# Layer 0's edge pass: one-hot selections built in pairs of tiles from bf16 locations

## The reference

```python
h = x @ W_w + W_b
row, col = (edge_index[0], edge_index[1])
e = h[row] @ a_src + h[col] @ a_dst + a_b
e = jax.nn.leaky_relu(e, negative_slope=0.01)
attention = jax.nn.softmax(e, axis=0)
out = jax.ops.segment_sum(attention * h[col], row, num_segments=N_NODES)
```

## Time and profile before

| | us |
|---|---|
| median of three runs (11213.9 to 11227.5) | 11218.07 |
| profiled execution, its time | 11216.49 |
| profiled execution, span of the core | 11214.7 |
| first weigh of the pass / last half of a weigh, starts | 2893.7 / 3919.0 |

### The profile page before, as it was taken

How to read it: one execution, slowest core, us unless ns; L and a number is a source line. 1 busy time by engine, 2 the same in 40 slices (tenths; PEclk the granted TensorE clock), 3 DMA queues, 4 the chain that set the end, 5 groups by cost and what they waited for, 6 DMA issues and landing times. The chain is left out here.

```text
span 11214.7 us, 161449 instructions
## 1 busy us (share of the span) xinstructions
PE 7016.7 (63%) x46023; PEld 5941.3 (53%) x46024; DVE 6329.4 (56%) x14524; ACT 2694.6 (24%) x4442; POOL 5210.9 (46%) x5267
## 2 busy tenths in 40 slices
PE   0034334443567658878787456666666588888885
PEld 0033333333466646666666334444444588888885
DVE  8932222222577766666666444444445566666665
ACT  5022222222455532222222132222222100000000
POOL 0057777777100057777777300000000477777773
PEclk5566666666678779999999779989898566666665
DMA  4045545545444445555555500000000333333335
GB/s 153 0 144 157 157 155 158 157 155 168 116 111 114 110 127 149 154 156 148 154 149 156 96 10 0 0 0 0 0 0 1 83 103 107 103 104 107 103 105 86
DMA packets 1150492, 1136.52 MB, mean 101 GB/s; under 512 B 239363, under 2 KB 959825, under 8 KB 1150117
## 3 DMA queue, kind: packets, MB, share of 16 engines
q1 hardware_dynamic: 948422, 666.82, 21.2%
q0 software_dynamic: 195904, 465.66, 15.2%
q10 hardware_dynamic: 6048, 2.84, 0.1%
HBM read 731.30 MB, written 403.51 MB: 101 GB/s over the span
## 5 line engine op out<-in xcount | busy, mean ns | idle before, releaser
L1028 POOL DMA_INDIRECT buf<-node_rows,buf x1728 | 1743.9, 1009 | 527.4 <-issue 526.2
L1522 POOL DMA_INDIRECT buf<-node_rows_ln,buf x1728 | 1711.4, 990 | 561.2 <-issue 496.9
L694 POOL DMA_INDIRECT edge_rows_by_src<-buf x1728 | 1692.6, 979 | 551.5 <-issue 526.4
L1058 PE MATMUL psum<-buf 128*128 128x128 f32 x1728 | 375.3, 375 | 1296.5 <-DVE buf L1021 1293.6
L2025 PE MATMUL psum<-parts,buf 128*128 x4896 | 1068.1, 368 | 141.4 <-issue 97.0
L2175 POOL IOTA buf<- 49x1 f32 x1 | 0.1, 124 | 2244.4 <-POOLq L821 2244.4
L1058 PEld LDWEIGHTS psum<-buf 128*128 128x128 f32 x1728 | 304.8, 199 | 1316.8 <-issue 1316.8
L2003 ACT CAST buf<-psum 128x1024 bf16<-128x1024 f32 x612 | 619.5, 1012 | 1475.7 <-PE psum L2014 1475.7
L786 DVE COPY buf<-buf 128x32 int32<-128x32 int32 x108 | 20.1, 186 | 1465.7 <-DMA buf<-records_by_dst 1465.5
L2041 DVE TENSOR_TENSOR buf<-buf,ends_of 128x2048 bf16<-128x2048 bf16 x614 | 724.6, 1222 | 134.5 <-issue 134.4
L2014 PE MATMUL psum<-buf 128*128 128x128 bf16 x4904 | 431.9, 235 | 569.0 <-DVE buf L2041 569.0
(11 more groups left out here) (428 smaller groups left out, 14529.8 us busy)
## 6 DMA issues: line engine op xcount, KB each, us to landing
buf<-edge_rows_by_src SPq DMA_DIRECT2D x114, 1056.0 KB, 5.7
buf<-edge_rows_by_src SPq DMA_DIRECT2D x110, 1024.0 KB
buf<-in_edge_attr SPq DMA_DIRECT2D x864, 128.0 KB
running_weighted_sums<-buf SPq DMA_DIRECT2D x108, 544.0 KB, 3.5
buf<-loc_rows_by_src SPq DMA_DIRECT2D x110, 512.0 KB, 5.0
buf<-loc_rows_by_dst SPq DMA_DIRECT2D x110, 512.0 KB, 4.8
running_sums<-buf SPq DMA_DIRECT2D x108, 512.0 KB, 3.0
edge_rows_by_src<-buf SPq DMA_DIRECT2D x139, 260.0 KB, 2.7
```

The costliest lines, as they stand in the source:

```text
L694: nc.gpsimd.indirect_dma_start(rows, bass.IndirectOffsetOnAxis(ap=at[:, h, t:t + 1], axis=0), st[:, h, t, :], None).then_inc(scattered[h], 16)
L1028: nc.gpsimd.indirect_dma_start(rows[:, t, 0:used], None, table, bass.IndirectOffsetOnAxis(ap=stage[:, t:t + 1], axis=0)).then_inc(sem, 16)
L1058: last = nc.tensor.transpose(psT[:, sg % 2, t * P:(t + 1) * P], oh[:, 4 * sg + t, :], c["ident"][:])
L1522: nc.gpsimd.indirect_dma_start(xn[:, j, t, :], None, table1, bass.IndirectOffsetOnAxis(ap=stage[:, j // 4, at:at + 1], axis=0)).then_inc(g ...
```

## The change

`iota` gets each number twice, next to each other. A new step `pick` copies the 32 locations of a unit into `locs`, bf16, and `compare` reads them from there, in a view of pairs. `sel` keeps two tiles of a pair interleaved, element by element (pair, location, tile of the pair). PE's turns read every second element of it. `weigh` reads `sel` in its new order, and writes `oh`, which keeps its old order (tile, location), through a permuted view. `pick` for unit n+2 stands ahead of `weigh` for unit n and now has the wait for the rows.

```diff
--- before.py
+++ after.py
@@ -1074,8 +1074,8 @@
     assert NU % R == 0 and NT + 2 * U <= NTX and GROUPS_U == 4
     with es:
         rows, oh = sb([P, R, U, W]), sb([P, U, P])
-        sel, turned_sel = sb([P, 2, U, P], BF16), sb([P, GROUPS_U, TURN, P], BF16)
-        iota, ident = sb([P, P], BF16), sb([P, P], BF16)
+        sel, turned_sel = sb([P, 2, U // 2, P, 2], BF16), sb([P, GROUPS_U, TURN, P], BF16)
+        iota, ident, locs = sb([P, P, 2], BF16), sb([P, P], BF16), sb([P, 2, U], BF16)
         ab, e1, e2, p = sb([P, 1]), sb([P, 2, U]), sb([P, 2, U]), sb([P, 2, U])
         mx, m1, mrun, mold, negm, fac = sb([P, 1]), sb([1, 1]), sb([1, 1]), sb([P, 1]), sb([P, 1]), sb([P, 2])
         psA = es.enter_context(nc.psum_tensor(fresh("psum"), [P, 2, 3, 512], F32))
@@ -1084,7 +1084,7 @@
         psS = psS_[:, 0:3 * U].rearrange("p (t k) -> p t k", k=3)
         highest, spread_max = psA[0:1, 1, 2, 2 * W:2 * W + P], psA[:, 1, 2, 2 * W + P:2 * W + P + 1]
         (loaded, saved, got0, got1, got2, numbered, hot, turned, evacuated, scored, maxed, max_turned, max_run, max_spread, newmax,
-         weights, weighted, summed, scaled, added, cleared, dve_chain) = (sem() for _ in range(22))
+         weights, weighted, summed, scaled, added, cleared, dve_chain, picked) = (sem() for _ in range(23))
         got = (got0, got1, got2)
         by_tile = stored.rearrange("(p t) c -> p t c", p=P)
         DV = 4
@@ -1153,7 +1153,8 @@
                     pe.wait_ge(hot, 2 * m + (g // 2 + 1))
                     pe.wait_ge(evacuated, 4 * m + g)
                     for t in range(TURN):
-                        last = nc.tensor.transpose(psT[:, t, :], sel[:, k, TURN * g + t, :], ident[:])
+                        at = TURN * g + t
+                        last = nc.tensor.transpose(psT[:, t, :], sel[:, k, at // 2, :, at % 2], ident[:])
                     last.then_inc(turned, 1)
 
                 def score(m, g, blocks):
@@ -1216,13 +1217,19 @@
 
             @block.vector
             def _(dve):
-                def compare(half, k, s, rows_at, weighed=None):
+                by_two = lambda v: v.rearrange("p (a t) -> p a t", t=2).unsqueeze(2)
+
+                def pick(n, k, s, rows_at):
+                    dve.wait_ge(got[s], rows_at)
+                    nc.vector.tensor_copy(locs[:, k, :].unsqueeze(2), rows[:, s, :, W - 2:W - 1]).then_inc(picked, 1)
+
+                def compare(n, half, k, weighed=None):
                     if half == 0:
-                        dve.wait_ge(got[s], rows_at)
+                        dve.wait_ge(picked, n + 1)
                     if weighed is not None:
                         dve.wait_ge(weighted, 2 * weighed + (half + 1))
-                    of = slice(half * HALF, (half + 1) * HALF)
-                    nc.vector.tensor_tensor(sel[:, k, of, :], bc(iota[:].unsqueeze(1), [P, HALF, P]), bc(rows[:, s, of, W - 2:W - 1], [P, HALF, P]),
+                    of = slice(half * PAIRS, (half + 1) * PAIRS)
+                    nc.vector.tensor_tensor(sel[:, k, of], bc(iota[:].unsqueeze(1), [P, PAIRS, P, 2]), bc(by_two(locs[:, k, half * HALF:(half + 1) * HALF]), [P, PAIRS, P, 2]),
                                             ALU.is_equal).then_inc(hot, 1)
 
                 def finalize(n, k, s):
@@ -1253,7 +1260,8 @@
                     dve.wait_ge(weights, n + 1)
                     for half in range(2):
                         of = slice(half * HALF, (half + 1) * HALF)
-                        nc.vector.tensor_tensor(oh[:, of, :], sel[:, k, of, :], bc(p[:, k, of].unsqueeze(2), [P, HALF, P]), ALU.mult).then_inc(weighted, 1)
+                        nc.vector.tensor_tensor(oh[:, of, :].rearrange("p (a t) k -> p a k t", t=2), sel[:, k, half * PAIRS:(half + 1) * PAIRS],
+                                                bc(by_two(p[:, k, of]), [P, PAIRS, P, 2]), ALU.mult).then_inc(weighted, 1)
 
                 def add(n, first_pair, done):
                     for half in range(2):
@@ -1268,7 +1276,7 @@
 
                 nc.vector.memset(c["idx"][:, NT:NTX], DUMMY)
                 nc.vector.memset(c["loc"][:, NT:NTX], -1.0)
-                nc.vector.tensor_copy(iota[:], c["iota"][:])
+                nc.vector.tensor_copy(iota[:], bc(c["iota"][:].unsqueeze(2), [P, P, 2]))
                 nc.vector.tensor_copy(ident[:], c["ident"][:]).then_inc(numbered, 1)
                 nc.vector.memset(mrun[:], NEG)
                 nc.vector.memset(negm[:], -NEG).then_inc(cleared, 1)
@@ -1276,22 +1284,25 @@
                 dve.wait_ge(loaded, 16)
                 dve.wait_ge(cleared, 1)
                 dve.wait_ge(numbered, 1)
-                compare(0, 0, 0, 32)
-                compare(1, 0, 0, 32)
+                pick(0, 0, 0, 32)
+                pick(1, 1, 1, 32)
+                compare(0, 0, 0)
+                compare(0, 1, 0)
                 finalize(0, 0, 0)
                 raise_max(0)
                 renew(0, again=False)
-                compare(0, 1, 1, 32)
-                compare(1, 1, 1, 32)
+                compare(1, 0, 1)
+                compare(1, 1, 1)
                 finalize(1, 1, 1)
                 with dve.Fori(0, NU // (2 * R)) as i:
                     for u in range(2 * R):
                         n = 2 * R * i + u
                         rows_at = 64 * i + 32 * ((u + 2) // R + 1)
+                        pick(n + 2, u % 2, (u + 2) % R, rows_at)
                         weigh(n, u % 2)
-                        compare(0, u % 2, (u + 2) % R, rows_at, n)
+                        compare(n + 2, 0, u % 2, n)
                         raise_max(n + 1)
-                        compare(1, u % 2, (u + 2) % R, rows_at, n)
+                        compare(n + 2, 1, u % 2, n)
                         renew(n + 1)
                         add(n, i * (4 * R * PAIRS) + 2 * u * PAIRS, i * (4 * R * PAIRS) + 2 * u * PAIRS)
                         finalize(n + 2, u % 2, (u + 2) % R)
```

## The result

| | us |
|---|---|
| the changed kernel, median of four runs (11303.51 to 11320.96) | 11309.2 |
| the kernel before, median beside them | 11216.41 |
| ratio, with its 95% interval | 1.0082 (1.0065 to 1.0100) |
| span of the changed kernel's profiled execution | 11319.1 |

What follows compares the result with a forecast made beforehand. After the edit each unit is bound by the circle weigh, spread, last total, row load, landing, pick: 20.81 us against 18.73. Six units +10.7, times nine +96, before the loop -2, transposes +2: 11314 us, range 11262 to 11352.

Steps and rivals of the forecast that it cites:

- Compares: DVE's two compares a unit drop from 2288 to 1222 ns each in bf16 pairs, saving 2.13 us a unit on DVE.
- Weigh: DVE's weigh writes hopping between two rows, 1.71 ns an element against 1.04: 3.65 us a half, +1.37.
- Pick: DVE's cast of 32 locations, 0.15 us; placed ahead of weigh, it takes along the wait for the rows.
- W to the spread maximum: From the unit's first weigh (W) to PE's spreading of the maximum (L1173): 8.47 us mean, +1.37, so 9.84.
- Landing 5.7: From SP issuing the second half's row load to the rows' arrival: 5.7 us, at least 5.5.
- Unit: One ordinary loop unit of 32 tiles, from W through spread, load, landing and pick to next W: 20.81 us against 18.73.
- Ahead of the loop: Before the loop two compare halves are waited for, so the quicker compares save 2 us.
- rival A: Weigh's write hops but rows land in time: about +57 us, 11275; chance 16%.
- the first kind: Units bound by weigh, PE, spread, renew and adds, alternating with DVE-bound ones; under in-time landing they grow 1.37 us.
- B: Hopping write is free, weigh stays 2284 ns, only the landing circle counts: +10 to +25 us, 11238; chance 9%.
- C: Hop free and rows landing in time, so the kernel is faster: -20 to -38 us, 11190; chance 5%.
- D: Hop costs much more, 2.5 ns an element, putting DVE in front: +210 us, 11428; chance 4%.

Runs made afterwards that it cites:

- slow_compare: The changed kernel without pick and bf16 locations: compare reads f32 locations from rows, weigh keeps its hopping write; 12928.93 us against 12793.19 before, ratio 1.0105.
- straight_write: The changed kernel with oh also kept in pairs, so weigh writes without a hop and PE reads strided weights; 11285.39 us, ratio 1.0060 to the kernel before.
- pick_behind: The changed kernel with pick for unit n+2 moved behind weigh for unit n in the loop; 11310.99 us, ratio 1.0084 to the kernel before.
- wait_alone: The kernel before with only DVE's wait for the rows of unit n+2 moved ahead of weigh for unit n; 11252.23 us against 11214.84, ratio 1.0031.
- filled_behind: The changed kernel with pick behind weigh, and PE's idle stretches filled with products nobody reads; ratio 1.0062 to the kernel before.
- straight_behind: The changed kernel with oh kept in pairs and written straight, and pick behind weigh; 11218.67 us, ratio 1.0004 to the kernel before.
- the two quarters: Straight write with pick behind weigh, plus weigh's first half and PE's total of it cut in two quarters; 12697.06 us against 12793.19 before, ratio 0.9930.

## Why the prediction came out

**The number.** 11314 forecast, 11309.2 measured, +96 against +93. The terms, by the steps of the prediction:

- *Compares*: 1222 ns forecast, a median of 1224 measured. Right, and worth some 53 us with the write in place (slow_compare).
- *Weigh*: 3.65 us forecast from 256-element rows, 3.76 measured: 1.76 ns an element. The mechanism was right, straight_write shows it; 0.11 too small.
- *Pick*: 188 ns, and 0.10 to the next instruction. Right.
- *W to the spread maximum*: 9.84 forecast, 9.76 on the mean of the units, in part by luck: PE's first total starts 1.48 us later, not 1.37, and takes 5.56 us where it took 5.82. *Load issued 5.07 later*: 5.06. *Landing 5.7*: 5.7. *Unit*: 20.81 forecast, 20.61 in the one shown and 20.2 to 21.1 in ordinary ones. The circle is as described, and pick's wait, forecast at 0.5 to 1 in most units, is 0.78 in 43 of the 54.
- *Ahead of the loop*: 2 us less forecast, 5.0 more measured, since pick(1) waits there ahead of compare(0). *Transposes*: 2 us forecast; eight turns take 0.61 us as before, so nothing is seen of them.

The loop was put at +96 and came to 91.1, and the rest at 0 against some 2 between the medians. Errors of a few us both ways went into that.

**What was not right behind the number.** The prediction treated that wait as a cost by itself: rival A was the same kernel with rows that land in time, at 11275. pick_behind is that kernel, and it takes 11311. What fails there is the growth of the first kind by 1.37, and in the forecast itself "mean of the two kinds W to L1173 is 8.47; +1.37": both hold PE's first total constant when everything around it moves. It does not stay: on the mean of the units it takes 5.82 us before, 5.56 in the changed kernel, 6.12 in wait_alone and 6.37 in pick_behind. The step from the changed kernel to pick_behind, 0.81 us, is as large as the landing wait. The four kernels with and without the hop (the write that alternates between two rows) and the wait have these passes: 1116.4 us with both, 1115.5 without the wait, 1087.3 without the hop, 1025.1 without either. Taking the wait away brings nothing while the hop is there and 62 us once it is gone; the two are not a sum. (In wait_alone the same wait costs 1.0031. In none of these is the clock steady, so each price holds what PE's first total did besides.) Why the wait is free beside the hop stays partly open: PE's clock takes its place in pick_behind, but with the clock held near 0.95 (filled_behind) most ordinary units did get shorter, 19.7 to 20.1 against some 20.3 us, while the pass did not, because of the units in which the clock fell back and of those behind the loop's turn.

**Rivals.** B (hop free) fell with weigh's 3763 ns, and its size was off too: straight_write, which has B's conditions but for PE's strided weights, gave 1.0060, not about 1.002. C (faster when hop and wait are both gone) had its conditions met in straight_behind, again but for the strided weights, and gave 1.0004 and not 0.998: by the terms shown there, most of what is missing went with those weights. C with weights read straight is not tested. D fell: 1.76 ns an element, not 2.5. The Trainium skill's 1.71 for a destination hopping 4 KiB ("Vector Engine (DVE) Microarchitecture Reference", section 5.2) stands near this case's 1.76 for a hop of 512 bytes, and its 2.50 for a step of 24 words is shown by no run here.

## What to carry to other kernels

A layout that makes a producer quick is paid by whoever writes out of it: before permuting a view, find a row of the trace whose write hops the same way, and move the permutation to the reader that pays least for it (PE took weights with a step of 8 bytes for 5% more time, where DVE's write cost 65% more), remembering that this too counts where the reader is on the path. When an instruction is placed ahead of another, its waits go with it; check the landing time against the new place, and do so ahead of the loop as well. And where PE runs at two levels, a time saved on another engine is not saved until PE's total has been looked at: shorten what PE waits for, as the two quarters did, rather than the engine that seems busiest.

## What the runs showed of the hardware

- A DVE product of 2048 f32 results takes 2284 to 2285 ns when neighbours are written next to each other, with its inputs read tile by tile (before) or in pairs (straight_write), and 3763 when they alternate between two rows 512 bytes apart.
- PE's granted clock in the pass is 0.74 to 0.81 in the kernels without filling (0.88 with the two quarters), and 0.95 to 0.97 with unread products in its idle stretches. 32 passes of the first total take 3.84 us where the clock stays high (4.04 with weights 8 bytes apart), and 5.1 to 6.8 in the kernels without filling.
- Raising the clock alone gave nothing (1.0001), and the quick compares with a straight write alone gave nothing (1.0004). Both together gave 0.9952.
